# Gate fold of the first batch and logits of the last batch from f16 parts, last logits two thirds into the last mix tile

## What is computed

```
x = x + tanh(g_xattn) * attention(layernorm(x), ctx)      # output through the mean of 8 We and Wo
hs = layernorm(x)
logits = hs @ w_gate                                      # 8 per token
best = argmax(softmax(logits)); gate = its probability
locations = cumsum(one_hot(best)) - 1                     # over all tokens, in order
kept = locations < 100
x = x + tanh(g_ffn) * gate * kept * (hs @ w_expert + b_expert)
```

## Time and profile before

| what | us |
|---|---|
| median of 3 runs | 416.38 |
| lowest, highest | 416.18, 416.67 |
| the profiled execution | 416.97 |
| its span (first to last instruction) | 415.5 |
| TensorE busy | 405.2 |
| VectorE busy | 332.8 |
| ScalarE busy | 227.6 |
| GpSimd busy | 166.2 |

### The profile page before, as it was taken

One profiled execution on the slowest core, in us unless ns is written; L12 is line 12 of the kernel. 1 busy time (PEld: TensorE's weight loads), 2 busy tenths in 40 slices (PEclk: granted clock), 3 DMA queues, 4 the chain that ended last, 5 costly groups with the idle time before them and its releaser, 6 DMA issues.

```text
span 415.5 us, 8770 instructions
## 1 busy us (share of the span) xinstructions
PE 405.2 (98%) x3122; PEld 191.7 (46%) x3122; DVE 332.8 (80%) x678; ACT 227.6 (55%) x318; POOL 166.2 (40%) x153
## 2 busy tenths in 40 slices
PE   8999999999999999999999999999999999999996
PEld 4566564444444344444434443443444444354442
DVE  7439346886797889988988998899896688579994
ACT  5435322569466754947585585748556473785100
POOL 2029999015080247309033530803261072550460
PEclk9999999999999999999999999999999999999999
DMA  8999971365058407723960683286059026231683
GB/s 266 340 390 396 390 291 35 89 120 161 2 113 184 174 0 163 213 96 88 174 208 2 141 227 101 65 175 232 2 128 235 6 51 175 71 115 34 118 175 137
DMA packets 64853, 63.19 MB, mean 152 GB/s; under 512 B 41225, under 2 KB 44437, under 8 KB 64811
## 3 DMA queue, kind: packets, MB, share of 16 engines
q1 hardware_dynamic: 59667, 56.18, 48.9%
q0 software_dynamic: 1632, 3.49, 3.1%
q10 hardware_dynamic: 3512, 2.97, 2.1%
HBM read 29.59 MB, written 12.98 MB: 102 GB/s over the span
## 4 chain that ended last, share of the span: by engine, by line
PE 78%; DVE 9%; POOL 4%; issue 4%; DMA 2%; ACT 1%; SPq 0%; DVEq 0%; POOLq 0%; ACTq 0%
PE ps L828 60%; PE ps L449 10%; PE ps L398 3%; PE ps L580 3%; DVE bn_raw L1450 2%; POOL known L1893 1%; POOL std L1902 1%; POOL rstd L1893 1%; DMA raw<-in_L_xattn_Wk_dram 1%; DMA q_stack<-shift 1%; DVE base_cnt L1619 1%; DVE rows L1789 1%; ACT xb L1215 1%; DVE bn_raw L1540 1%; DVE xb L1534 1%
## 5 line engine op out<-in xcount | busy, mean ns | idle before, releaser
L1215 ACT ACTIVATE probs<-ps 120x1024 f32<-120x1024 f32 x64 | 62.0, 1023 | 22.6 <-PE ps L828 22.6
L1568 DVE TENSOR_REDUCE neg_max<-ps 128x16 bf16<-128x1920 f32 x32 | 68.6, 2144 | 4.1 <-PE ps L828 4.1
L1952 POOL TENSOR_TENSOR attn_lo<-attn,attn_hi 128x512 f16<-128x512 f32 x28 | 31.8, 1157 | 95.9 <-ACT attn_hi L1215 95.9
L828 PE MATMUL ps<-xnT_hi,wqT_hi 128*128 128x512 f16 x128 | 48.6, 380 | 0.0
L828 PE MATMUL ps<-mixT_hi,attn_hi 128*128 128x512 f16 x128 | 48.6, 380 | 0.0
L828 PE MATMUL ps<-mixT_lo,attn_hi 128*128 128x512 f16 x128 | 48.5, 379 | 0.0
L828 PE MATMUL ps<-xnT_lo,wqT_hi 128*128 128x512 f16 x128 | 48.5, 379 | 0.0
L1960 POOL TENSOR_TENSOR xb<-xb,mix_bias 128x512 f32<-128x512 f32 x32 | 39.6, 1270 | 18.7 <-DVE cb_col L1511 18.7
L1215 ACT ACTIVATE q_hi<-ps,bias_cols 128x512 f16<-128x512 f32 x32 | 22.0, 687 | 35.3 <-PE ps L828 35.3
L828 PE MATMUL ps<-q_stack,k_stack 97*120 97x512 f16 x128 | 34.7, 390 | 0.9 <-DMA q_stack<-shift 0.8
L828 PE MATMUL ps<-probs,den_sel 120*32 120x256 f32 x512 | 34.1, 384 | 0.0
(11 more groups left out here) (270 smaller groups left out, 791.7 us busy)
## 6 DMA issues: line engine op xcount, KB each, us to landing
xb<-in_x_dram SPq DMA_DIRECT2D x8, 1024.0 KB, 6.0
q_stack<-q_hi SPq DMA_DIRECT2D x48, 128.0 KB
out_dram<-xb SPq DMA_DIRECT2D x6, 1024.0 KB, 6.0
raw<-in_L_xattn_We_dram SPq DMA_DIRECT2D x5, 1024.0 KB, 11.1
q_stack<-q_lo SPq DMA_DIRECT2D x32, 128.0 KB
xb<-in_L_xattn_We_dram SPq DMA_DIRECT2D x3, 1024.0 KB, 10.4
k_stack<-k_scratch SPq DMA_DIRECT2D x8, 360.0 KB, 4.3
out_dram<-xb SPq DMA_DIRECT2D x8, 256.0 KB, 2.1
```

The lines of the kernel that those rows point to most:

```text
L828: return e.matmul(out_, a, b, start=start, stop=stop, **kw)
L1215: return e.activation(out_, in_, func, **kw)
L1568: e.tensor_reduce(neg_max[:, :, :, g], quad[:, :, 0:NT * SK].rearrange("p j (t s) -> p t j s", t=NT), AX.X, ALU.max, negate=True).then_inc ...
L1952: e.tensor_tensor(attn_lo[:, g, :], attn[:, g, :], attn_hi[:, g, :], ALU.subtract).then_inc(s_alo, 1)
```

## The change

In the prologue, `gateT` is evacuated as two f16 parts: ScalarE writes `part_hi`, and VectorE, which had no work in this unit, writes `part_lo`. `gate_mix` then takes eight f16 matmuls by `gate_sum16` in place of four f32 ones by `gate_sum`. `gate_sum16` is 16 times `gate_sum`, so the scales of `gate_mix_high` and `gate_mix_low` get the factor `PART_SCALE` (1/16). VectorE's list of the first run gets `late_unit(5)` for the new evacuation.

In batch 7, `logits` takes the f16 path of batches 0 to 5; batch 6 keeps f32. The semaphore counts skip batch 6. ScalarE gets `part_high` ahead of `x2_high`, VectorE gets `part_low` between `moment2(1)` and `row_lo(6)`, and on TensorE `logits` moves from between mix tiles 2 and 3 to behind the eight high steps of tile 3.

```diff
             unit("gateT", pe, needs_of("wog", "mix_bias") + [(s_ws, NE - 1)],
-                 act=lambda e, b: e.activation(partT[:, :], b[:, :], ACT.Copy, scale=gate_scale[:, 0:1]))
+                 act=lambda e, b: e.activation(part_hi[:, :], b[:, :], ACT.Copy, scale=gate_scale[:, 0:1]),
+                 dve=lambda e, b: e.scalar_tensor_tensor(out=part_lo[:, :], in0=b[:, :], scalar=gate_scale[:, 0:1],
+                                                         in1=part_hi[:, :], op0=ALU.mult, op1=ALU.subtract))
...
-                    fold(e, g0_b).then_inc(s_mg, 1)
+                    for k in range(NK):
+                        for part in (part_hi, part_lo):
+                            ins = mm(g0_b[:, k * NE:(k + 1) * NE], part[:, k * P:(k + 1) * P], gate_sum16[:, NE:2 * NE],
+                                     start=(part is part_hi), stop=(part is part_lo))
+                    ins.then_inc(s_mg, 1)
...
-                if b < B - 2:
-                    e.wait_ge(s_pth, b + 1)
-                    e.wait_ge(s_ptl, b + 1)
+                if b != B - 2:
+                    n = b + 1 if b < B - 2 else B - 1
+                    e.wait_ge(s_pth, n)
+                    e.wait_ge(s_ptl, n)
...
-                (mix_high, 0, 2), (mix_low, 0, 2), (logits, 0, 0), (mix_high, 0, 3), (mix_low, 0, 3),
+                (mix_high, 0, 2), (mix_low, 0, 2), (mix_high, 0, 3), (logits, 0, 0), (mix_low, 0, 3),
...
-                            scale=ATTN_SCALE * MIX_SCALE).then_inc(s_mgh, 1)
+                            scale=ATTN_SCALE * MIX_SCALE * PART_SCALE).then_inc(s_mgh, 1)
...
-                (x2_high, 0, 0), (x2_high, 0, 1), (x2_high, 0, 2), (x2_high, 0, 3), (gate_exp, 0, 0),
+                (part_high, 0, 0), (x2_high, 0, 0), (x2_high, 0, 1), (x2_high, 0, 2), (x2_high, 0, 3), (gate_exp, 0, 0),
...
-                e.wait_ge(s_pth, b + 1)
+                e.wait_ge(s_pth, b + 1 if b < B - 2 else B - 1)
...
-                                           scalar=ATTN_SCALE * MIX_SCALE, in1=route_hi[:, 1, :, NE:2 * NE],
+                                           scalar=ATTN_SCALE * MIX_SCALE * PART_SCALE, in1=route_hi[:, 1, :, NE:2 * NE],
...
-                (scale_bias, 1, 0), late_unit(4),
+                (scale_bias, 1, 0), late_unit(4), late_unit(5),
...
-                (x1_tile, 0, 1), (route_sum, 0, 0), (stats2, 0, 1), (moment2, 0, 1), (row_lo, 0, 6),
+                (x1_tile, 0, 1), (route_sum, 0, 0), (stats2, 0, 1), (moment2, 0, 1), (part_low, 0, 0), (row_lo, 0, 6),
```

## The result

The changed kernel is slower by about a quarter of a per cent: ratio 1.0023, 95% interval 1.0016 to 1.0031; medians 417.63 us over 13 runs against 416.57 over 13 of before. On the first median of 416.38 the ratio is +0.96 us (0.67 to 1.29). Forecast were +0.97 and the direction.

A forecast was written before the change was run, and what follows sets the result against it. TensorE was taken to bound the middle of batch 0 and VectorE's full queue the tail; 0.37 + 0.60 = 0.97 us on the median 416.38 gave 417.35 us, range 416.6 to 417.9.

The forecast's parts named there:

- The tail: Batch 7: part_low in VectorE's full queue delays choose and places by 0.60 us; TensorE's won us is spent waiting.
- the 0.37: Batch 0, part 1 in total: weight_sums(0, 2) starts 0.37 us later, at 104.24; bounds +0.12 and +0.47.
- The fold: TensorE, batch 0: eight f16 matmuls take 0.20 us where four f32 ones took 0.81, saving 0.61.
- VectorE's step: Prologue: part_lo waits for part_hi, begins at 94.24 and moves stats1 of batch 2 1.03 us later.
- Route (a): TensorE, batch 0: weight_sums(0, 0) waits for part_lo through prologue_over, 0.73 us later; less the 0.61 saved, +0.12.
- Route (b): Batch 0: 1.03 us passes through stats1, rstd1, normalise1 and x_hi to exp(0, 3), on which weight_sums(0, 2) waits until 104.24.
- The end of tile 3: TensorE, batch 7: mix tile 3 ends near 387.06 where it ended near 388.10, one us won.
- Rival E: Last batch: TensorE, not VectorE, sets the end, so 1.09 us comes out; 415.66 us, chance 0.04.
- Rival C: Last batch: part_low fits into VectorE's queue for nothing; 416.75 us, chance 0.08.
- Rival D: Part 1 gives its 0.61 us and neither delay counts, needing prologue_over to be free; 416.37 us, chance 0.06.
- Rival B: Batch 0: ScalarE's delay is hidden, for instance because x_hi did not wait on its input; 417.10 us, chance 0.08.
- Rival F: Tail: TensorE's clock falls in the pause ahead of places, up to 13.2 us more; 417.4 to 430.6, chance 0.04.

The follow-up runs named there:

- the run without the prologue wait: Kernel before with only the f16 gate fold, weight_sums(0, 0) not waiting for the new VectorE step and route_x(1) waiting for it instead; ratio 0.9985 (0.9972 to 0.9999).
- the unused step: Kernel before with part_high and part_low issued in the last batch but read by nothing, logits still f32 at their old place; ratio 1.0009 (0.9998 to 1.0021).
- the second one: Kernel before with part_high, part_low and another instruction of part_low's form, all unread; places at 18.98 behind route_attn; ratio 1.0048 (1.0022 to 1.0073), size not used.
- the mended kernel: Changed kernel with the gate's low part in VectorE's gap and out of the prologue wait, places behind row_product 7; ratios against before 0.9953, again 0.9956.

## Why the prediction was right, point by point

The sum was 0.37 + 0.60 = 0.97 us; the positions give 0.28 + 0.55 = 0.83 and the times 0.96 (0.67 to 1.29). The tail was right in size and cause. In front the new step's start and the wait that it lengthens were right, but most of the 0.37 was put on a wait that does not exist.

The fold: taken at 0.20 us from the batch logits, measured 0.20. VectorE's step: taken to begin 1.03 behind `mixT_lo`, measured 1.03 (93.72 to 94.75).

Route (a), the prologue wait, was right in kind and 0.15 short: taken at 0.73, measured 0.88, since the handover from VectorE to TensorE took 0.20 (95.50 to 95.70) and not 0.05.

Route (b) was wrong in the step that joined it to TensorE: "`weight_sums(0, 2)` waits for it", said of `exp(0, 3)`. ScalarE's delay was there (`x_hi` 7.40 behind the gate unit, 6.37 before), but the run without the prologue wait shows the group starting 0.69 ahead of that exponential's end, and even in the changed kernel it starts 0.03 ahead of it. In the changed kernel nothing of route (b) reaches TensorE; route (a) alone gives 0.88 - 0.61 = 0.27 of the 0.28. The two errors, 0.15 too little in (a) and a route (b) that does not hold, nearly met: (a) as predicted would have given +0.12, and the forecast of +0.37 came from (b). The total was right partly by that luck.

The tail: taken at 0.60, measured 0.55, as the new step's pitch was 0.58 and `route_sum` stood 0.03 nearer to `route_attn` (2.81 and 2.84). That TensorE's us would end in a wait ahead of `places` was right: "waits 1.9 us" was 1.67 of idle time in the row, 1.83 from the end of `row_product` 6 by its steps. On the way there two slips nearly cancelled. The end of tile 3, "near 387.06", comes out if the last row is counted by its length, and the 388.10 it is held against by its steps; by steps it would have been 386.90, 1.20 us won. But the f16 logits had to wait 0.21 us for `part_lo` (it ended at 386.31, they started at 386.46, the high steps were through at 386.25), a wait that the prediction left out. So 0.98 was won. Neither slip could reach the end, as that time only goes into the wait ahead of `places`.

Rival E (TensorE sets the tail) is refuted by the unused step and by the f32 logits moved alone. Rival C (a free slot in VectorE's queue) is refuted by the unused step and by the second one. Rival D needed the prologue wait to be free, and it cost 0.88. Rival B, at 417.10, said that ScalarE's delay does not count, which is what happened in the changed kernel; only the reason it offered, that `x_hi` might not wait for its input, was wrong. In front it was nearer to the mechanism than the forecast, and had a chance of 0.08.

Rival F, the clock, did not come in. Behind the pause ahead of `places` the granted clock is 1.00 (start and end of the stretch, us, busy (instructions) of TensorE, its weight loads, VectorE, ScalarE and GpSimd, granted clock, DMA share, GB/s), the same level as in the earlier trace rows:

```profile
399.71:412.94 13.23, 13.21 (x62) 5.87 (x62) 9.89 (x20) 0.00 (x0) 4.84 (x5) 1.00 0.67 182
```

The Trainium skill (TensorE: Matmul & The Clock Gate, "The HAM clock gate") has an idle TensorE fall to 1.2 GHz; this pause shows none of it, and the last section has one behind which it did.

## What to carry to other kernels

When an f32 matmul is cut into f16 parts, the price is the evacuation that is added, not the matmuls. Here that was VectorE's low part, both times; ScalarE's high part took the place of an old step in front and ran in idle time in the tail. So ask which engine writes the low part, whether its queue is full there, and who waits for a count that the new step joins (here a wait on "all of the prologue", which grew by one step without being edited).

A wait on a count has to be followed to the step that makes this count: the mistake in this prediction was one count on `s_ex`, `exp(0, 3)` taken for `exp(0, 2)`.

And an engine that gains time ahead of a wait on a full engine has gained nothing until the wait itself is moved: on the path, moving `places` by one row product was worth 1.87 us in the changed kernel, and 0.36 us without the gain.

## What the runs showed of the hardware

A pause of TensorE and its clock. In the second run of the changed kernel TensorE stood still for 2.56 us between batch 7's last value sums and the first row product, 1.00 us shortly ahead of it, with ScalarE and VectorE waiting too (for something that the trace calls remote). First the idle time of TensorE:

```profile
366.40 0.56 PE L1153 MATMUL ps<-ident,xb 100*128 100x100 f32 x4 [1.00 <-issue]
366.90 1.06 PE L830 MATMUL ps<-probs,v_all 120*32 120x512 f32 x8
370.52 0.38 PE L830 MATMUL ps<-wqT_hi,xnT_hi 128*128 128x512 f16 x1 [2.56 <-issue]
```

of ScalarE and of VectorE:

```profile
369.88 0.50 ACT L1222 ACTIVATE xnT_hi<-ps 128x400 f16<-128x400 f32 x1 [2.43 <-remote]
369.13 1.76 DVE L1525 RECIPROCAL rden<-ps 128x256 f32<-128x256 f32 x1 [2.29 <-remote]
```

then busy time by stretch of the same kernel, with the columns as above (the granted clock is the last but two):

```profile
370.00:371.00 1.00, 0.47 (x3) 0.27 (x4) 1.00 (x2) 0.38 (x1) 0.55 (x1) 0.98 0.45 98
371.00:372.00 1.00, 1.00 (x4) 0.39 (x3) 0.32 (x1) 0.65 (x2) 0.00 (x0) 0.50 0.66 164
372.00:373.00 1.00, 1.00 (x3) 0.30 (x2) 0.00 (x0) 1.00 (x2) 0.00 (x0) 0.50 0.32 131
373.00:374.00 1.00, 1.00 (x6) 0.74 (x5) 0.49 (x1) 0.05 (x1) 0.00 (x0) 0.50 0.00 0
374.00:375.00 1.00, 1.00 (x7) 0.57 (x6) 0.00 (x0) 0.60 (x2) 0.00 (x0) 0.81 0.00 0
```

The granted clock is 0.50, the 1.2 GHz level, from 371 to 374, and 128x512 steps start 0.43 us apart instead of 0.22. It fell only after TensorE had gone back to work, and was up again before 375, with TensorE busy all the while. The first run of the mended kernel has the same two pauses (1.00 and 2.58 us) at the same place, and 0.50 behind them as well. What TensorE waited for there is open.

The landing of one small transfer. In batch 6 the row `q_stack<-shift` is the last thing that the scores of batch 7 wait for. In the profile of before they start here:

```profile
351.27 1.04 PE L828 MATMUL ps<-q_stack,k_stack 97*120 97x512 f16 x4 [0.85 <-DMA q_stack<-shift]
```

From issue to landing the row took 4.21 us; this is its piece of the chain that ended last:

```profile
346.71 4.21 DMA q_stack<-shift
```

In the changed kernel with `places` moved, with nothing edited near it:

```profile
346.72 4.98 DMA q_stack<-shift
```

Over the fourteen profiles it took from 3.58 to 4.98 us, 4.06 in that of the changed kernel. The scores of batch 7 stand 258.96 us behind the gate unit in the profile of before, 259.03 in the changed kernel, and 259.94 with `places` moved.

This spread hides what happens in front. Ahead of it, at the logits of batch 6, the front is still exact: 254.75 or 254.76 behind the gate unit in all four profiles with the new fold and the prologue wait, 254.46 to 254.58 in the six with the old fold. Behind it, at `route_attn` of batch 7, the six with the old fold stand at 288.14, 288.25, 288.28, 288.38, 288.65 (the profile of before) and 289.85, and of the four others those of the changed kernel and of the fold alone at 288.55 and 288.58. So the profile of before is a late one, which is why the pair in the section on the result shows +0.45 and not 0.83, and the other two of the four, at 289.47 and 294.43, are later still. That the 0.28 arrives at the end in most executions fits these numbers and the measured 0.96, but is not shown one by one. A spread of over a us is more than each half of the change is worth, and helps to explain why single halves could not be told from no change by time alone.
